# Two tables of partial neighbour sums in place of four in a graph kernel: each accumulating scatter waits for the second one ahead of it

## The chip, the cores and the metric

The kernel runs on one core of one Trainium2 chip. The metric is the device time of one execution in microseconds (us); before the change it is 12705.93 us, the median of 3 runs.

## The reference

12500 nodes of 128 features, 412500 edges sorted by `dst` (a self loop for each node among them), an `edge_weight` and 64 edge features for each edge. Two layers:

```
relevant = segment_sum(x[dst] * edge_weight[:, None], src, 12500)     # layer 0: the neighbour sums
x = layernorm(x + relevant @ W1 + (relevant * x) @ W2)
q, k, v = x @ Wq + bq, x @ Wk + bk, x @ Wv + bv                        # layer 1: attention, 8 heads
e = edge_attr_64 @ We + be
attn = softmax over the edges of each dst of (q[dst] . (k[src] + e)) / 4
x = layernorm(x + segment_sum(attn * v[src], dst) @ Wo + bo)
```

The neighbour sums of layer 0 are gathered by `dst` (sorted, so 128 edges in a row read a short window of `x`) and added up by `src` (random rows). That adding up is the part that the change touches.

## The kernel before, in words

Edges go in tiles of 128; eight tiles (`G`) are a group, and there are 403 groups (`NG`), so 3224 tiles. Five stages follow one another, each a block in which the engines run their own instruction streams and meet through semaphores.

**prepare** (L159 to L329) loads the edge arrays, derives the start row of each tile and the marks of the attention stage, and stores them. On SyncE's queue (L206 to L250) the order is: loads, `dst_pad` and its two shifted read-backs, then the zero fill of every table `rel_sum[r]` (L228 to L231: four transfers of `zeros` for each table), then `src_flat`, `starts`, `firsts`, `rel_flat`, the four `marks` and the two `whole`. The stage ends when all of them have landed (L250).

**neighbours** (L332 to L478) runs once over the 403 groups. For each group SyncE broadcasts the `src` values into `src_bc` (L375) and loads eight windows of `x` (L380). VectorE builds `same` and `spread` (L396, L400) and the eight columns of target rows, `row` (L414). TensorE multiplies them into `coef_ps` (L427), ScalarE copies it (L449), TensorE makes `sum_ps` (L436), ScalarE copies it into `sums` (L455). GpSimd then issues eight indirect DMAs (L471), one for each tile: 128 rows of 512 B from `sums[:, b, j]` are added to the rows of a table that `row[:, b, j]` names. Two of these may name the same row of the result, and an accumulating DMA reads its destination before it writes it, so two that may overlap in time must have different tables or be ordered. Scatter j goes to table j % REPLICAS, each table has its own semaphore `added[r]`, and before each scatter GpSimd waits until the one before it on the same table has landed. With four tables that is the scatter four ahead:

```
r, before = j % REPLICAS, j // REPLICAS
if j % 4 == 0:
    pool.wait_ge(sum_out, s.g * 2 + j // 4 + 1)
wait_alone(pool, added[r], (s.g * PER + before) * 16, passed)
pool.indirect_dma_start(out=rel_sum[r], ..., compute_op=ALU.add, ...).then_inc(added[r], 16)
```

`wait_alone` (L77 to L81) is a wait with a semaphore increment behind it; the wait and the increment are one instruction in the trace, under L81. The buffers `row` and `sums` are double: VectorE before L414 and ScalarE before L455 wait until all scatters of the group before the last have landed (L412, L451).

**nodes_one** (L528 to L676) goes over the nodes in 25 steps of 512. SyncE loads `xb` and a slice of each table into `rep` (L582, L584), VectorE adds the slices (L598, L599, L602), multiplies by `xb` (L605), and TensorE, ScalarE and VectorE make the layer norm and q, k, v. GpSimd stores them.

**attention** (L701 to L1168) is the long second pass over the 403 groups, and **nodes_two** (L1171 to L1264) ends the kernel. Neither touches the tables.

Of the kernel before, what the change touches and what calls it, by code (L numbers as in the profile page):

```python
# [25 lines left out]
ALU = mybir.AluOpType  # L26
# [2 lines left out]

P = 128  # L30
G = 8
REPLICAS = 4
BIG = 1.0e30
EPS = 1.0e-5
NB = 4 * P
# [34 lines left out]
def wait(eng, sem, value):  # L70

    if isinstance(value, int) and value <= 0:
        return
    eng.wait_ge(sem, value)  # L74
# [22 lines left out]
def build_gnn(nc, x, src, dst, edge_attr, edge_weight, W1, W2, Wq, bq, Wk, bk, Wv, bv, We, be, Wo, bo, out):  # L97
# [25 lines left out]
    firsts = nc.dram_tensor("firsts", (TP,), I32).ap()  # L123
    rel_sum = [nc.dram_tensor(f"rel_sum{r}", (N + P, D), F32).ap() for r in range(REPLICAS)]
    x1_rows = nc.dram_tensor("x1_rows", (N, D), F32).ap()
# [33 lines left out]
def prepare(nc, e):  # L159
# [13 lines left out]
    with ExitStack() as ctx:  # L173
# [24 lines left out]
        with nc.Block() as block:  # L198
# [7 lines left out]
            def _(sp):  # L206
# [20 lines left out]
                sp.wait_ge(zeroed, 1)  # L227
                for r in range(REPLICAS):  # L228
                    table = rel_sum[r].rearrange("n d -> (n d)").rearrange("(z p k) -> z p k", z=4, p=P)
# [15 lines left out]
                with nc.allow_non_contiguous_dma(reason="one word for each tile, once"):  # L245
# [3 lines left out]
                                 ).then_inc(prep_stored, 16)  # L249
                sp.wait_ge(prep_stored, 16 * (4 * REPLICAS + 10))  # L250

# [80 lines left out]
def neighbours(nc, e):  # L332
# [5 lines left out]
    with ExitStack() as ctx:  # L338
# [3 lines left out]
        def sem(name):  # L342
            return ctx.enter_context(nc.semaphore(name))
# [17 lines left out]
        coef_done, coef_out, sum_done, sum_out = (sem(n) for n in ("coef_done", "coef_out", "sum_done", "sum_out"))  # L361
        added = [sem(f"added{r}") for r in range(REPLICAS)]
        PER = G // REPLICAS

        with nc.Block() as block:
# [19 lines left out]
            def _(dve):  # L385
# [3 lines left out]
                def body(s):  # L389
# [21 lines left out]
                    dve.wait_ge(rows_b, s.g + 1)  # L411
                    for r in range(REPLICAS):  # L412
                        wait(dve, added[r], 16 * PER * (s.g - 1))
# [88 lines left out]
def layer_norm(nc, ch, i, passed, y, stats, mv, rstd, var_ready, rooted, out, done):  # L502

    for j in range(4):
        ch.mark(nc.vector.bn_stats(stats[:, j, :], y[:, j, :]))  # L505
    ch.settle()
    ch.eng.sem_inc(passed, 1)
    for j in range(4):
        ch.mark(nc.vector.bn_aggr(mv[:, j, :], stats[:, j, :]))  # L509
    ch.settle()  # L510
    nc.vector.tensor_scalar(rstd[:, 0, :], mv[:, :, 1], EPS, None, ALU.add).then_inc(var_ready, 1)  # L511
    ch.eng.wait_ge(rooted, i + 1)
    ch.link(nc.vector.reciprocal(rstd[:, 2, :], rstd[:, 1, :]))  # L513
    for j in range(4):
        nc.vector.tensor_scalar(out[:, j, :], y[:, j, :], mv[:, j, 0:1], rstd[:, 2, j:j + 1],  # L515
                                ALU.subtract, ALU.mult).then_inc(done, 1)


def node_steps(eng, N, body):

    full = N // NB
    body(0, 0)
    with eng.Fori(1, full) as i:  # L523
        body(i, i * NB)
    body(full, N - NB)


def nodes_one(nc, e):  # L528

    N, D = e["N"], e["D"]  # L530
# [3 lines left out]
    with ExitStack() as ctx:  # L534
        def sb(name, shape, dt=F32):
            return ctx.enter_context(nc.sbuf_tensor(name, shape, dt))
# [4 lines left out]
        def sem(name):  # L541
            return ctx.enter_context(nc.semaphore(name))
# [4 lines left out]
        xb = sb("xb", [P, 4, D])  # L547
        rep = sb("rep", [P, REPLICAS, 4 * D])
        pair = sb("pair", [P, 2, 4, D])
        half_sum = sb("half_sum", [P, 2, 4 * D])  # L550
        pair_t = sb("pair_t", [P, 2, 4, P])
        y = sb("y", [P, 4, D])
        stats = sb("stats", [P, 4, 6])
# [8 lines left out]
        w_in, bias_ready, in_x, summed, pair_turned, pair_out, y_done = (sem("n1_" + n) for n in (  # L562
            "w_in", "bias_ready", "in_x", "summed", "pair_turned", "pair_out", "y_done"))
        var_ready, rooted, x1_ready, x1_turned, x1_out, qkv_done, qkv_ready, stored, ch1 = (sem("n1_" + n) for n in (
            "var_ready", "rooted", "x1_ready", "x1_turned", "x1_out", "qkv_done", "qkv_ready", "stored", "chain"))
        CH = 2 + 1 + 4 + 4 + 1

        with nc.Block() as block:
            @block.sync
            def _(sp):  # L570
                for i, w in enumerate((e["W1"], e["W2"])):
                    sp.dma_start(w12[:, i, :], w).then_inc(w_in, 16)
                for i, w in enumerate((e["Wq"], e["Wk"], e["Wv"])):
                    sp.dma_start(wqkv[:, i, :], w).then_inc(w_in, 16)
                for i, b in enumerate((e["bq"], e["bk"], e["bv"], e["be"])):
                    sp.dma_start(bias[:, i, :], b.rearrange("(a d) -> a d", a=1).to_broadcast([P, D])
                                 ).then_inc(w_in, 16)

                def body(i, row0):
                    wait_alone(sp, x1_ready, i * 4, e["passed"])  # L580
                    rows = bass.ds(row0, NB)
                    sp.dma_start(xb[:], x[rows, :].rearrange("(p j) d -> p j d", j=4)).then_inc(in_x, 16)  # L582
                    for r in range(REPLICAS):
                        sp.dma_start(rep[:, r, :], rel_sum[r][rows, :].rearrange("(p j) d -> p (j d)", j=4)  # L584
                                     ).then_inc(in_x, 16)

                node_steps(sp, N, body)

            @block.vector
            def _(dve):  # L590
                dve.wait_ge(w_in, 9 * 16)
                nc.vector.tensor_tensor(bias[:, 1, :], bias[:, 1, :], bias[:, 3, :], ALU.add).then_inc(bias_ready, 1)
                dve.wait_ge(bias_ready, 1)

                def body(i, row0):
                    ch = Chain(dve, ch1, CH, i)
                    dve.wait_ge(in_x, (i + 1) * 16 * (1 + REPLICAS))
                    ch.mark(nc.vector.tensor_tensor(half_sum[:, 0, :], rep[:, 0, :], rep[:, 1, :], ALU.add))  # L598
                    ch.mark(nc.vector.tensor_tensor(half_sum[:, 1, :], rep[:, 2, :], rep[:, 3, :], ALU.add))  # L599
                    ch.settle()  # L600
                    wait(dve, pair_turned, i * 2)
                    nc.vector.tensor_tensor(pair[:, 0].rearrange("p j d -> p (j d)"), half_sum[:, 0, :],  # L602
                                            half_sum[:, 1, :], ALU.add).then_inc(summed, 1)
                    dve.wait_ge(summed, i * 2 + 1)
                    nc.vector.tensor_tensor(pair[:, 1], pair[:, 0], xb[:], ALU.mult).then_inc(summed, 1)  # L605
                    dve.wait_ge(y_done, i + 1)
                    ch.link(nc.vector.tensor_tensor(y[:], xb[:], y_ps[:], ALU.add))
                    wait(dve, stored, i * 48)
                    layer_norm(nc, ch, i, e["passed"], y, stats, mv, rstd, var_ready, rooted, x1, x1_ready)
                    for j in range(4):  # L610
                        dve.wait_ge(qkv_done, i * 4 + j + 1)
                        nc.vector.tensor_tensor(qkv[:, j], qkv_ps[j][:, 0:3, :], bias[:, 0:3, :], ALU.add
                                                ).then_inc(qkv_ready, 1)
                    ch.close()

                node_steps(dve, N, body)
# [554 lines left out]
def nodes_two(nc, e, acc):  # L1171

    N, D, x1_rows, out = e["N"], e["D"], e["x1_rows"], e["out"]
    with ExitStack() as ctx:
# [3 lines left out]
        def sem(name):  # L1178
# [15 lines left out]
            "w_in", "in_x", "att_ready", "y_done", "y_read", "var_ready", "rooted", "res_ready", "stored", "chain"))  # L1194
        CH = 1 + 1 + 4 + 4 + 1

        with nc.Block() as block:
# [13 lines left out]
            def _(dve):  # L1211
                dve.wait_ge(w_in, 32)

                def body(i, row0):
                    ch = Chain(dve, chain, CH, i)
                    nodes = bass.ds(row0, NB)
                    ch.link(nc.vector.reciprocal(inv[:], acc[:, 1, nodes]))  # L1217
                    wait(dve, y_done, i)
                    nc.vector.tensor_tensor(att[:], acc[:, 0, nodes], inv[:], ALU.mult).then_inc(att_ready, 1)  # L1219
                    dve.wait_ge(in_x, (i + 1) * 16)  # L1220
                    nc.vector.tensor_tensor(xo[:], xb[:], bo[:].rearrange("p (a d) -> p a d", a=1)
                                            .to_broadcast([P, 4, D]), ALU.add).then_inc(y_read, 1)
                    dve.wait_ge(y_read, i + 1)
                    dve.wait_ge(y_done, i + 1)
                    ch.link(nc.vector.tensor_tensor(y[:], xo[:], y_ps[:], ALU.add))  # L1225
                    wait(dve, stored, i * 16)
                    layer_norm(nc, ch, i, e["passed"], y, stats, mv, rstd, var_ready, rooted, res, res_ready)
                    ch.close()
# [58 lines left out]
```

## Time and profile before

| | us |
|---|---|
| median of 3 runs | 12705.93 (12699.51 to 12716.78) |
| span of the profiled execution | 12688.7 |
| of it: scatters, from the first to the last | 210.6 to 6201.4 |
| of it: nodes_one | about 6208 to 6740 |
| of it: attention | about 6740 to the last half per cent of the span |

The profiled execution has no time of its own beside its span; the span lies 17.2 us under the median of the runs. Busy shares of the whole span: TensorE's matmuls 66%, GpSimd 64%, VectorE 45%, ScalarE 35%. They are averages over stages with different limits: in the scatter stage TensorE is busy for about four tenths of each slice and GpSimd for eight, in the attention stage TensorE for nine tenths or more.

### The profile page before, as it was taken

The numbers are of one execution on the slowest core, as the hardware profiler recorded it, in microseconds if no ns is written. First come the engines' busy times: TensorE is split into PE (matmuls) and PEld (weight loads), VectorE is DVE, ScalarE is ACT, GpSimd is POOL, SyncE is SP. The second block draws the span as 40 slices with busy tenths as digits, with TensorE's granted clock in tenths as the row PEclk, the third lists the DMA queues.
The fourth block names the chain that finished last, engine by engine and source line by source line (L and its number), as shares of the span: only waits on it lengthen the run. The fifth ranks groups of instructions, "written<-read, shape, count | busy, mean of one in ns | idle before, by whom it ended". The sixth has DMA issues, their size and how long they took to land. (4 is left out here: it accounts for less than half of the span.)

```text
span 12688.7 us, 238906 instructions
## 1 busy us (share of the span) xinstructions
PE 8350.0 (66%) x54376; PEld 7719.8 (61%) x54376; DVE 5700.1 (45%) x23624; ACT 4480.1 (35%) x8672; POOL 8152.3 (64%) x6563
## 2 busy tenths in 40 slices
PE   2444444444444444444457999999999999999992
PEld 1343343443443343343336998999999989989892
DVE  2333333333333333333344555555555555555557
ACT  1111111111111111111104666666666666566660
POOL 2888888888888888888504555555555555555550
PEclk6666666666666666666657889999988898898995
DMA  7666666666666666666435666666666666666661
GB/s 199 105 106 106 105 106 106 105 106 106 105 106 106 105 106 106 105 106 106 95 114 157 178 177 181 178 179 182 180 176 179 176 181 179 175 181 175 182 182 50
DMA packets 2256479, 1764.21 MB, mean 139 GB/s; under 512 B 727631, under 2 KB 1990545, under 8 KB 2253937
## 3 DMA queue, kind: packets, MB, share of 16 engines
q0 software_dynamic: 628608, 667.05, 31.9%
q1 hardware_dynamic: 1627507, 1094.03, 30.0%
q14 instruction: 345, 2.83, 0.1%
q8 instruction: 19, 0.31, 0.0%
HBM read 1476.50 MB, written 283.60 MB: 139 GB/s over the span
## 5 line engine op out<-in xcount | busy, mean ns | idle before, releaser
L471 POOL DMA_INDIRECT rel_sum<-sums,row x3224 | 5008.9, 1554 | 1190.1 <-issue 648.9
L877 POOL DMA_INDIRECT kv<-kv_rows,src_idx x3224 | 3064.8, 951 | 2568.8 <-DVE msg L1076 1314.2
L427 PE MATMUL coef_ps<-same,spread 128*128 128x128 f32 x6448 | 1631.9, 437 | 3567.1 <-DVE spread L400 2963.4
L427 PEld LDWEIGHTS coef_ps<-same,spread 128*128 128x128 f32 x6448 | 1422.1, 325 | 3743.0 <-DVE spread L400 3129.2
L1090 DVE TENSOR_TENSOR acc<-acc,out_ps 128x256 f32 x3224 | 1335.4, 414 | 1050.2 <-PE out_ps L968 954.2
L414 DVE TENSOR_TENSOR row<-moved,src_col 128x8 int32<-128x8 f32 x403 | 70.3, 175 | 3787.2 <-DMA rel_sum<-sums,row 3787.1
L966 PE MATMUL out_ps<-put,msg 128*128 128x128 f32 x6448 | 1615.0, 340 | 88.9 <-DVE acc L1090 31.2
L968 PE MATMUL out_ps<-put,weight 128*128 128x128 f32 x6448 | 1516.1, 324 | 0.0
L455 ACT ACTIVATE sums<-sum_ps 128x512 f32<-128x512 f32 x806 | 437.7, 594 | 2895.4 <-DMA rel_sum<-sums,row 2893.9
L966 PEld LDWEIGHTS out_ps<-put,msg 128*128 128x128 f32 x6448 | 1243.2, 239 | 185.6 <-issue 77.3
L449 ACT ACTIVATE coef<-coef_ps 128x512 f32<-128x512 f32 x806 | 481.3, 597 | 2307.2 <-PE coef_ps L427 2306.1
L968 PEld LDWEIGHTS out_ps<-put,weight 128*128 128x128 f32 x6448 | 1247.8, 240 | 0.0
L400 DVE TENSOR_SCALAR spread<-iota_n,rel_col,w_col 128x128 f32<-128x128 f32 x3224 | 1213.1, 381 | 0.0
L396 DVE SCALAR_TENSOR_TENSOR same<-src_bc,src_col,later 128x128 f32<-128x128 f32 x3224 | 1119.2, 347 | 178.0 <-DVE row L414 163.2
L915 PE MATMUL ke_ps<-attr_t,we 128*128 128x128 f32 x6448 | 1096.0, 275 | 0.0
L915 PEld LDWEIGHTS ke_ps<-attr_t,we 128*128 128x128 f32 x6448 | 998.4, 195 | 0.0
L436 PE MATMUL sum_ps<-x_win,coef 128*128 128x128 f32 x6448 | 996.3, 320 | 0.0
L436 PEld LDWEIGHTS sum_ps<-x_win,coef 128*128 128x128 f32 x6448 | 995.8, 242 | 0.0
L1123 ACT ACTIVATE put<-iota_n,neg_rel 128x128 f32<-128x128 f32 x3224 | 981.1, 387 | 0.0
L913 PE MATMUL ke_ps<-ident,kv 128*128 128x128 f32 x3224 | 902.8, 280 | 7.8 <-ACT attr_t L1132 7.8
L924 PE MATMUL misc_ps<-head_of,prod 128*128 128x8 f32 x6448 | 842.9, 259 | 95.6 <-DVE prod L1001 95.6
L924 PEld LDWEIGHTS misc_ps<-head_of,prod 128*128 128x128 f32 x6448 | 815.2, 199 | 135.2 <-DVE prod L1001 107.8
(151 smaller groups left out, 10350.2 us busy)
## 6 DMA issues: line engine op xcount, KB each, us to landing
src_bc<-src_flat SPq DMA_DIRECT2D x403, 512.0 KB, 4.2
x_win<-in_x SPq DMA_DIRECT2D x3224, 64.0 KB
rel_bc<-rel_flat SPq DMA_DIRECT2D x403, 512.0 KB
q_win<-q_rows SPq DMA_DIRECT2D x3224, 64.0 KB
attr<-in_edge_attr SPq DMA_DIRECT2D x402, 256.0 KB
rel_sum<-sums,row POOLq DMA_INDIRECT x3224, 3.4
kv<-kv_rows,src_idx POOLq DMA_INDIRECT x3224
mark<-marks SPq DMA_DIRECT2D x403, 128.0 KB
```

The source lines that it names most:

```text
L396: nc.vector.scalar_tensor_tensor(out=same[:, b, j, :], in0=src_bc[:, b, j * P:(j + 1) * P], scalar=src_col[:, t], in1=later[:], op0=ALU.is ...
L400: nc.vector.tensor_scalar(spread[:, b, j, :], iota_n[:], rel_col[:, t], w_col[:, t], ALU.is_equal, ALU.mult).then_inc(masks, 1)
L427: last = nc.tensor.matmul(coef_ps[k][:, i, :], spread[:, b, j, :], same[:, b, j, :], start=True, stop=True)
L436: last = nc.tensor.matmul(sum_ps[k][:, i, :], coef[:, b, j, :], x_win[:, b, j, :], start=True, stop=True)
L471: pool.indirect_dma_start(out=rel_sum[r], out_offset=bass.IndirectOffsetOnAxis(ap=row[:, b, j:j + 1], axis=0), in_=sums[:, b, j, :], in_of ...
L877: pool.indirect_dma_start(out=kv[:, b3, j, :], out_offset=None, in_=kv_rows, in_offset=bass.IndirectOffsetOnAxis(ap=src_idx[:, b3, j:j + 1 ...
L915: mm = nc.tensor.matmul(ke_ps[k][:, i, :], we2[:, j % 2, :], attr_t[:, j // 2, :], start=False, stop=True)
L924: mm = nc.tensor.matmul(logit_ps[:, j * H:(j + 1) * H], prod[:, j * P:(j + 1) * P], head_of[:], start=True, stop=True)
L966: nc.tensor.matmul(out_ps[p2 % 2][:, i, 0, :], msg[:, j, :], put[:, c.turn(2), j, :], start=True, stop=True)
L968: mm = nc.tensor.matmul(out_ps[p2 % 2][:, i, 1, :], weight[:, j, :], put[:, c.turn(2), j, :], start=True, stop=True)
L1090: nc.vector.tensor_tensor(win, win, out_ps[j // 2 % 2][:, j % 2, :, :], ALU.add).then_inc(summed, 1)
L1123: nc.scalar.activation(put[:, n.turn(2), j, :], iota_n[:], ACT.Abs, bias=neg_rel[:, bass.ds(n.g * G + j, 1)]).then_inc(put_dist, 1)
```

## The change

`REPLICAS` goes from 4 to 2. What follows from it in the code: two tables are zeroed in place of four (8 transfers on SyncE's queue in place of 16); scatter j goes to table j % 2, so it waits for the scatter two ahead of it; `PER`, the scatters of a group on one table, goes from 2 to 4; `nodes_one` loads two slices of tables in place of four, and one addition in place of three makes the sum.

```
-REPLICAS = 4
+REPLICAS = 2
...
-        half_sum = sb("half_sum", [P, 2, 4 * D])
...
-        CH = 2 + 1 + 4 + 4 + 1
+        CH = 1 + 4 + 4 + 1
...
                     dve.wait_ge(in_x, (i + 1) * 16 * (1 + REPLICAS))
-                    ch.mark(nc.vector.tensor_tensor(half_sum[:, 0, :], rep[:, 0, :], rep[:, 1, :], ALU.add))
-                    ch.mark(nc.vector.tensor_tensor(half_sum[:, 1, :], rep[:, 2, :], rep[:, 3, :], ALU.add))
-                    ch.settle()
                     wait(dve, pair_turned, i * 2)
-                    nc.vector.tensor_tensor(pair[:, 0].rearrange("p j d -> p (j d)"), half_sum[:, 0, :],
-                                            half_sum[:, 1, :], ALU.add).then_inc(summed, 1)
+                    nc.vector.tensor_tensor(pair[:, 0].rearrange("p j d -> p (j d)"), rep[:, 0, :],
+                                            rep[:, 1, :], ALU.add).then_inc(summed, 1)
```

## Rows read from the trace of the kernel before

**Rows 1.** The page: span; costliest groups (busy us, mean ns, idle before and its releaser).

```profile
span 12688.7 us, 238906 instructions
...
L471 POOL DMA_INDIRECT rel_sum<-sums,row x3224 | 5008.9, 1554 | 1190.1 <-issue 648.9
...
L455 ACT ACTIVATE sums<-sum_ps 128x512 f32<-128x512 f32 x806 | 437.7, 594 | 2895.4 <-DMA rel_sum<-sums,row 2893.9
```

**Rows 2.** Windows: the scatter stage, nodes_one, attention and the end.

```profile
210.00:6205.00 5995.00, 2542.01 (x12864) 2366.63 (x12864) 1947.44 (x10843) 916.98 (x1609) 5008.88 (x3224) 0.67 0.62 105
6208.00:6740.00 532.00, 301.19 (x900) 197.98 (x900) 205.93 (x576) 51.20 (x101) 50.60 (x77) 0.59 0.34 112
6740.00:12688.00 5948.00, 5485.87 (x40502) 5140.40 (x40502) 3488.52 (x12140) 3493.83 (x6880) 3089.64 (x3256) 0.88 0.63 172
```

**Rows 3.** Timeline of one group's middle: start, duration, engine, line, idle before.

```profile
2727.56 1.59 POOL L471 DMA_INDIRECT rel_sum<-sums,row  x1 [0.30 <-issue]
2729.45 1.55 POOL L471 DMA_INDIRECT rel_sum<-sums,row  x1 [0.30 <-issue]
...
2730.82 0.33 SPq L375 DMA_DIRECT2D src_bc<-src_flat  x1
...
2731.31 1.55 POOL L471 DMA_INDIRECT rel_sum<-sums,row  x1 [0.30 <-DMA rel_sum<-sums,row]
```

**Rows 4.** Line L471, 1000 to 6000 us: duration ns, first and last start, landing.

```profile
L471 POOL DMA_INDIRECT rel_sum<-sums,row x2691: 1542/1548/1698, 998.6 to 5999.1; - x193
...
DMA to landing us min/median/max: 3.2/3.4/6.1
```

**Rows 5.** Line L471 in four windows of one scatter: starts 2725.7, 2729.5, 2733.2, 2736.9.

```profile
L471 POOL DMA_INDIRECT rel_sum<-sums,row x1: 1544/1544/1544, 2725.7 to 2725.7; - x1
DMA to landing us min/median/max: 3.3/3.3/3.3
...
L471 POOL DMA_INDIRECT rel_sum<-sums,row x1: 1550/1550/1550, 2729.5 to 2729.5; - x1
DMA to landing us min/median/max: 4.5/4.5/4.5
...
DMA to landing us min/median/max: 3.2/3.2/3.2
...
DMA to landing us min/median/max: 3.5/3.5/3.5
```

**Rows 6.** Line L81 on GpSimd's queue, 2733.5 to 2736: when waits are passed.

```profile
L81 POOLq EVENT_SEMAPHORE  x2: 17/17/17, 2734.0 to 2735.5; - x2
```

**Rows 7.** A gather of the attention stage: the wait passed, then its start.

```profile
L81 POOLq EVENT_SEMAPHORE  x1: 17/17/17, 7999.8 to 7999.8; - x1
...
8000.57 0.95 POOL L877 DMA_INDIRECT kv<-kv_rows,src_idx  x1 [3.03 <-DVE msg L1076]
```

**Rows 8.** Line L471 from 208 to 216 us: first issue and first scatters.

```profile
L471 POOLq MOVE  x4: 29/29/29, 209.6 to 211.6; - x4
L471 POOL DMA_INDIRECT rel_sum<-sums,row x3: 1552/1569/1901, 210.6 to 214.6; - x3
```

**Rows 9.** prepare: SyncE's queue and VectorE in order of time; transfers of zeros.

```profile
48.65 34.48 SPq L231 DMA_DIRECT2D rel_sum<-zeros  x16
...
86.48 33.42 SPq L235 DMA_DIRECT2D starts<-start_ti  x1
...
140.33 19.51 SPq L243 DMA_DIRECT2D marks<-mark_t  x4
...
84.30 7.07 DVE L297 TENSOR_TENSOR_SCAN mark_t<-next_t,mark_t 128x3328 f32<-128x3328 int32 x1
...
rel_sum<-zeros SPq DMA_DIRECT2D x16, 1578.5 KB, 27.9
...
GB/s 0 0 79 317 313 278 143 157 43 295 352 447 414 432 417 432 419 429 419 429 417 434 414 354 91 2 2 0 221 348 348 348 348 95 1 1 0 0 341 90
```

**Rows 10.** nodes_one on VectorE by line: busy, mean ns, idle before.

```profile
L599 DVE TENSOR_TENSOR half_sum<-rep 128x512 f32<-128x512 f32 x25 | 17.1, 685 | 0.0
L598 DVE TENSOR_TENSOR half_sum<-rep 128x512 f32<-128x512 f32 x25 | 17.0, 682 | 3.0 <-DMA rep<-rel_sum 3.0
```

## The prediction, made before the changed kernel had run

> **What bounds the kernel now.** I read the page's costliest groups first, then the windows by stage, then the timeline of one group and the landing times of single scatters. The stages run one after the other, so each has a limit of its own. The change touches prepare, the scatter stage and nodes_one, not attention, which is TensorE's: 5486 of its 5948 us are matmuls [rows 2]. I expect attention unchanged.
>
> In the scatter stage GpSimd is busy 5009 of 5995 us and nothing else comes near it [rows 2]. The reader should see what its idle time is: before nearly every scatter stands the same 0.30 us, put down to issue or to a landing that falls into that gap, and one scatter starts 1.85 us after the other, which is 1.55 of duration and 0.30 of gap [rows 3]. The mean over the stage is 1.859 us: the first scatter starts at 210.6 [rows 8], the last of the 3224 at 6201.4 (the table of times), and 5990.8 / 3223 = 1.859. A group of eight takes 14.87 us. The others wait for the scatters: ScalarE's copy into `sums` stands idle 2894 us for landings [rows 1], about 7 us for each of the 403 groups. So GpSimd's own instruction rate is the limit, and the landings are not: the waits on `added` are met early.
>
> How early decides this case. A scatter lands 3.4 us after its start by the median, never under 3.2, at most 6.1 [rows 4]. With four tables, scatter i waits for one that started 4 x 1.859 = 7.4 us before it. That leaves 4.0 us, in which GpSimd's queue runs ahead: at 2734.0 the wait on the scatter of 2729.45 is passed, 4.5 us after that one's start and 2.9 us before the scatter behind the wait starts, at 2736.9 [rows 3, 5, 6].
>
> **The change part by part.**
>
> (a) The wait. Now scatter i waits for the landing of i-2. The cost is not landing against 2 x 1.859 = 3.72 us alone: between the passing of a wait and the start of the DMA behind it lies the time in which the queue handles the instruction. Today the queue has that time in hand; with the wait ending late it stands in line with the landing. The trace of before doesn't show it for a steady scatter. The nearest rows: a gather with GpSimd idle starts at 8000.57, 0.8 us after its wait was passed at 7999.8 [rows 7]; the first scatter starts 1.0 us after its register move (209.6 to 210.6), which itself follows the wait by up to 0.1 [rows 8]. So it is between 0.8 and 1.1 us. I take 0.9, the gather's value and the register move that a scatter has in addition; the first scatter also ran long (1.90 against 1.55 us), so it looks like a cold start.
>
> A pair of scatters then costs landing + 0.9, where today it costs 3.72. In a quiet stretch: 3.3 + 0.9 = 4.2 us. Not all are quiet: of the four scatters in rows 5 the landings are 3.3, 4.5, 3.2 and 3.5 us. The 4.5 is that of the scatter that started at 2729.45, while SyncE issued the 512 KB broadcast `src_bc` at 2730.82 [rows 3]; the scatter behind it, started at 2731.31, was late as well, its wait being passed at 2735.5, so 4.2 us [rows 6]. There is one such broadcast and one burst of eight window loads in each group, before and after the change.
>
> The scatters form two chains, one for each table: tiles 1, 3, 5, 7 and tiles 0, 2, 4, 6. The odd chain takes 14.5 us of landings (3.3 + 4.5 + 3.2 + 3.5) and 4 x 0.9 = 3.6, together 18.1 us for each group. The even one has the 4.2 and three of about 3.4: 14.4 + 3.6 = 18.0. They share GpSimd, and which is the later one changes, so I add an estimated 0.2: 18.3 us against 14.87. For 403 groups: 3.43 x 403 = +1382 us. With 0.8 in place of 0.9 it would be 161 less (4 x 0.1 x 403), with 1.1 it would be 322 more.
>
> What is queued behind the waiting scatter: GpSimd's queue holds nothing but the next scatters. Who waits for them: `row` and `sums` need the landing of the last scatter of the group before the last. They get it one group ahead of use; ScalarE's 2894 us of idle show 7 us of slack in each group [rows 1], and a group that takes 18.3 us makes that slack longer. SyncE's loads wait for VectorE and TensorE, which move with them. So nothing new comes late, and PE's, VectorE's and ScalarE's work stays hidden under the scatters.
>
> The Trainium skill, "DMA: Bandwidth & Descriptors", section "Anatomy of one DMA", gives a DMA issued by GpSimd as about 2.0 us plus its bytes over 436 GB/s, an estimated 2.15 us for 64 KB. Counted from issue, 2.15 + 0.9 is under 3.72 and (a) would cost nothing; the trace has no landing under 3.2 us [rows 4], so it disagrees. Counted from the end of the 1.55 us on GpSimd, it would be 3.7 us, 0.4 above the quiet landings here, and (a) would cost 4 x 0.4 x 403 = 645 us more than my sum; the trace has 3.4 - 1.55 = 1.85.
>
> (b) The zero fill. 16 transfers of 1578.5 KB; DMA moves some 425 GB/s in that stretch, so 3.8 us each [rows 9]. SyncE's queue is in line behind them: `starts` needs 33.4 us to issue, because the queues are full [rows 9]. Eight fewer: -30.4 us. It is on the path, since the stage ends with the last transfer of that queue. The next limit is VectorE's last scan, which ends at 91.4, while the marks are issued at 140.3 and would then be at 109.9 [rows 9]: still behind it, so all 30 us are kept.
>
> (c) nodes_one. VectorE's two additions of 0.68 us go from each of 25 steps, with their settling wait: 2 x 0.68 = 1.37, and about 0.04 for the wait [rows 10]. They are on the path, because they stand right behind the q, k, v additions of the step before with no idle (only 3.0 us in all 25, in the first step). The loads of `rep` are hidden under that step but in the first one, where two fewer issues save about 1. Together -36 us. The least it can be is 0, if a load of `rep` landed as late as the additions end now; the 3.0 us of idle in 25 steps speak against that.
>
> Sum against the profiled execution: 12688.7 + 1382 - 30 - 36 = 14,005 us of span; with the 17 us between span and median, 14,022. I forecast 14,020 us, 10.3% slower.
>
> **The rivals.**
>
> *The wait stays hidden (not slower).* If a wait that ends late needed only the 0.30 us that stands before each scatter now, the link in a quiet stretch would be 3.3 + 0.3 = 3.6 us, under 3.72, and GpSimd's rate would remain the limit; the broadcasts' excess would have to be made up too, by other landings. Then only (b) and (c) count: 12706 - 66 = 12,640 us. For it: the 0.30 is all that a reader sees between scatters [rows 3]. Against it: the 0.8 of the gather [rows 7] and a 4.5 in every group, which by itself leaves 4.5 + 0.3 - 3.72 = 1.1 us. It decides from landing plus handling at 3.72. Chance 0.03.
>
> *The broadcasts don't hurt.* With fewer scatters in flight and a longer period, the late landings might fade to the quiet 3.3. Pair 4.2, scatter 2.1 us: (2.1 - 1.859) x 3224 = +777, less 66: 13,417 us. For it: most landings are quiet. Against: the broadcast is as large as before and one comes in each group. Chance 0.14.
>
> *The chains hurt each other, or handling is as long as the first scatter shows.* With 1.1 us: 19.1 us for a group, +1705 - 66: 14,345. Or with 0.9, where the late landing of one chain also holds up the other by its 0.9 excess: 19.2, 14,385. Chance 0.16.
>
> The likeliest is my sum with its neighbours, from 13,860 (handling 0.8) to 14,250, halfway to the case above: 0.66. 0.01 is left for something that I don't see.
>
> **How the numbers follow.** All cases but the first are slower by over 0.2% (about 25 us, what a measurement of this kernel can tell from no change): slower 0.96. The first is faster: 0.03, and 0.01 for same. The range: 0.2 may stay out. The hidden case (0.03) does, and so do the lower half of the fading case and the upper part of the last: 13,400 to 14,400 us.
>
> **What the profile of the changed kernel would show.** For (a): the scatters' duration still 1.55 us, but idle before them 0.7 us and more, released by landings of `rel_sum`; starts 4.2 us apart for every second one and 18.3 us for a group; the stage 7375 us long; GpSimd busy 68% of it in place of 84%. Right or wrong on the handling time: wait passed to start, 0.9. For (b): first scatter at about 180. For (c): nodes_one 36 us shorter. Attention at 5948. I would be wrong if that idle stayed at 0.30, if landings under the slower rate became much shorter than 3.3, or if the late ones spread to the whole group.

## The result, and the profile after

The changed kernel takes 13944.75 us (median of 3 runs, 13942.82 to 13958.27) against 12705.93: a ratio of 1.0976, 95% interval 1.0961 to 1.0991, slower. The forecast was 14,020.

The page of the changed kernel: the span, the two groups that answer to [rows 1], and the scatters' issue with its median landing.

```profile
span 13956.6 us, 238726 instructions
...
L471 POOL DMA_INDIRECT rel_sum<-sums,row x3224 | 5007.8, 1553 | 2505.6 <-issue 1175.2
...
L455 ACT ACTIVATE sums<-sum_ps 128x512 f32<-128x512 f32 x806 | 437.7, 594 | 4199.6 <-DMA rel_sum<-sums,row 4198.3
...
rel_sum<-sums,row POOLq DMA_INDIRECT x3224, 3.3
```

The scatters' own time did not move (5009 to 5008 us, 1.55 us each), nor did their median landing (3.4 and 3.3 us; those views hold half of the tiles each, and over all of them it is 3.40 and 3.35). The idle time before them more than doubled, from 1190 to 2506 us. Without the wait before the very first scatter (207 and 178 us) it is 984 and 2327 us: that difference, 1344 us, is the loss of the stage. ScalarE's copy into `sums` waits 4198 us instead of 2894: it has more slack, not less, as a follower of the scatters should.

Windows of the changed kernel (the scatter stage, nodes_one, attention). The columns, as in [rows 2]: stretch and its length; busy us and instructions of TensorE's matmuls, its weight loads, VectorE, ScalarE and GpSimd; granted clock of TensorE, busy share of the DMA engines, GB/s.

```profile
182.00:7518.00 7336.00, 2558.66 (x12864) 2367.05 (x12863) 1931.61 (x10840) 916.93 (x1609) 5007.83 (x3224) 0.64 0.51 86
7520.00:7970.00 450.00, 250.50 (x900) 162.99 (x900) 173.99 (x526) 51.20 (x101) 50.26 (x75) 0.74 0.32 103
8030.00:13685.00 5655.00, 5453.40 (x40164) 5123.03 (x40162) 3272.71 (x11664) 3469.74 (x6823) 3036.28 (x3200) 0.89 0.65 177
```

Beside [rows 2]: GpSimd is busy 5008 of 7336 us, 68%, where it was 84%. In nodes_one TensorE was granted 0.74 of its full clock, where it was 0.59. That I had not foreseen.

The timeline of one group's middle shows where the idle sits; compare [rows 3], where it was 0.30 us everywhere.

```profile
3014.75 1.59 POOL L471 DMA_INDIRECT rel_sum<-sums,row  x1 [0.80 <-DMA rel_sum<-sums,row]
3016.15 0.33 SPq L375 DMA_DIRECT2D src_bc<-src_flat  x1
3016.64 1.54 POOL L471 DMA_INDIRECT rel_sum<-sums,row  x1 [0.30 <-issue]
3020.20 1.55 POOL L471 DMA_INDIRECT rel_sum<-sums,row  x1 [2.01 <-DMA rel_sum<-sums,row]
...
3022.05 1.54 POOL L471 DMA_INDIRECT rel_sum<-sums,row  x1 [0.30 <-issue]
3024.51 1.55 POOL L471 DMA_INDIRECT rel_sum<-sums,row  x1 [0.92 <-DMA rel_sum<-sums,row]
```

The landing of the first of these alone, and GpSimd's wait on it (line L81):

```profile
L471 POOL DMA_INDIRECT rel_sum<-sums,row x1: 1587/1587/1587, 3014.8 to 3014.8; - x1
...
DMA to landing us min/median/max: 4.6/4.6/4.6
...
L81 POOLq EVENT_SEMAPHORE  x1: 17/17/17, 3019.4 to 3019.4; - x1
```

These lines show the mechanism. The scatter of 3014.75 has the broadcast of `src_bc` issued on top of it at 3016.15 and lands after 4.6 us. At that moment, 3019.4, the wait behind it is passed, and the next scatter on its table starts at 3020.20, 0.8 us later. From the start of one scatter to the start of the next on its table, which I call a link, it is 5.45 us; with four tables the same late landing cost nothing. In the quiet link after it, 3020.20 to 3024.51, it is 4.31 us instead of 3.72. The scatter in between (3022.05) starts 1.85 us behind its neighbour: GpSimd's own rate (1.55 us of duration and 0.30 of gap) still spaces the two that come together, and idle gathers before every second one. In this group the late scatter is tile 2; in most groups it is tile 3, as over all 403 groups tile 2 lands after 3.35 us by the median and tile 3 after 4.54.

The issues of line L471 over the whole run, with their first and last start, and the landings:

```profile
L471 POOL DMA_INDIRECT rel_sum<-sums,row x3224: 1537/1547/1836, 182.5 to 7515.9; - x190
...
DMA to landing us min/median/max: 3.1/3.3/5.3
```

(7515.9 - 182.5) / 3223 = 2.275 us for a scatter, 18.20 us for a group, against 1.859 and 14.87.

By stage, both profiled executions (the times are the starts of the first and last scatter of line L471 and of the first and last of attention's additions into `acc`):

| us | before | after | difference | forecast |
|---|---|---|---|---|
| to the first scatter | 210.6 | 182.5 | -28 | -30 |
| first to last scatter | 5990.9 | 7333.4 | +1343 | +1382 |
| last scatter to attention's first addition | 600.7 | 514.3 | -86 | -36 |
| attention, first to last addition | 5614.4 | 5654.5 | +40 | 0 |
| to the end | 272.1 | 272.0 | 0 | 0 |
| span | 12688.7 | 13956.6 | +1268 | +1316 |

The medians differ by 1239 us, 29 less than the spans. The last 272 us are nodes_two, which is 2% of the span and not the half per cent that the table of times before gave it. The 40 us of attention can't be laid to the change: that stage took 5614 to 5655 us in nine profiled executions of kernels that are alike in it, the changed kernel itself 5630 in another. But the three of them with the fast scatter stage took 5614 to 5621 us and the six with a slower one 5622 to 5655, so that a small effect is not excluded either.

### The profile page after: what moved, and what is told of

It reads as the page before. It is cut to its first block and busy times, and to the rows that moved or that the text cites. A ratio compares the mean times of both kernels' runs of the same rounds, so it can differ in the third digit from the quotient of the medians.

```text
span 13956.6 us, 238726 instructions
## 1 busy us (share of the span) xinstructions
PE 8363.3 (60%) x54376; PEld 7738.0 (55%) x54376; DVE 5653.7 (41%) x23574; ACT 4481.0 (32%) x8672; POOL 8145.9 (58%) x6563
## 5 line engine op out<-in xcount | busy, mean ns | idle before, releaser
L471 POOL DMA_INDIRECT rel_sum<-sums,row x3224 | 5007.8, 1553 | 2505.6 <-issue 1175.2
```

The source lines that it names most:

```text
L471: pool.indirect_dma_start(out=rel_sum[r], out_offset=bass.IndirectOffsetOnAxis(ap=row[:, b, j:j + 1], axis=0), in_=sums[:, b, j, :], in_of ...
```

## The experiments

Eleven runs follow: nine kernels, one of them twice, and the changed kernel once more. Four of them (the wait alone, nodes_one alone, the zero fill undone and three tables) ran together on a chip on which attention took 8350 us instead of some 5640, so that the kernel before took 15432.57 us there (median of 17 runs); their scatter stages and steps of nodes_one agree with those on the other chips to within half a per cent where the kernels are alike in them. Why attention is slow there is open. These four are compared with the kernel before on the same chip, and stage by stage.

**The wait alone.** Four tables, with the wait moved to the second scatter ahead:

```
-                        wait_alone(pool, added[r], (s.g * PER + before) * 16, passed)
+                        wait_alone(pool, added[(j - 2) % 4], (s.g * PER + (j + 2) // 4) * 16, passed)
```

> Four tables as before the change, but each scatter also waits for the landing of the second one ahead of it: part (a) alone. The wait on the fourth one ahead is replaced, since the nearer wait covers it in order. My theory (a link is landing plus a fixed 0.86 us of handling): the scatter stage grows as in the changed kernel, by some 1340 us, to 18.2 us for a group; zero fill and nodes_one as before; 14,050 us. Rival 1: part of the stage's loss comes of two scatters in a row hitting the same two tables, not of the wait; then the stage here is shorter than 18.0 us for a group, under 13,970. Rival 2: nodes_one's gain in the changed kernel (20.4 to 17.1 us a step) comes from what the slower scatter stage does to TensorE's clock; then its step is shorter here too, about 18.5, and the time about 14,000.

Measured: 16783.57 us, ratio 1.0879 (1.0863 to 1.0895), +1351 us. The scatter stage took 7337 us, 18.21 us for a group. Once more, beside the changed kernel on one ordinary chip:

> Part (a) alone once more, beside the changed kernel on one chip. Theory: before plus 1345 us; the scatter stage 7335 us, nodes_one's step 20.4 us; above the changed kernel by the 28 us of prepare and the 85 us of nodes_one, some 110 us. Rival: the two tables themselves matter and the difference is not between 90 and 130.

> The changed kernel as it is, on the same chip as the other three: before plus 1240 us (ratio 1.0976 on another occasion).

Measured: before 12718.62 (11 runs), the wait alone 14106.84 (ratio 1.1088, 1.1070 to 1.1107), the changed kernel 13986.62 (ratio 1.1003, 1.0984 to 1.1023). The wait alone on that chip, by its scatters and by nodes_one from 7603 to 8095 us:

```profile
L471 POOL DMA_INDIRECT rel_sum<-sums,row x3224: 1536/1546/1872, 213.4 to 7581.3; - x190
...
7603.00:8095.00 492.00, 290.66 (x868) 189.42 (x868) 197.79 (x554) 49.19 (x97) 48.24 (x72) 0.58 0.34 114
```

The scatter stage is 7368 us with four tables and 7377 with two (7563.5 - 186.3) on the same chip. So the wait makes the loss; that the same two tables are hit in turn adds no more than the 9 us between these traces. The two kernels differ by 120 us, where prepare and nodes_one should make some 110. The medians of the changed kernel on the two occasions, 13945 and 13987, show how far chips differ; the ratios overlap.

**nodes_one alone.** Two slices loaded and added, all else with four tables, so that the output lacks the sums of the other two:

```
-                    for r in range(REPLICAS):
+                    for r in range(2):
                         sp.dma_start(rep[:, r, :], rel_sum[r][rows, :]...
```

> Four tables, all zeroed and scattered to as before, but nodes_one reads and adds two of them only, as in the changed kernel (the output lacks the sums of the other two tables): part (c) alone. My prediction's theory: two additions fewer, 1.4 us a step, 36 us in all, 12,670 us. Rival, from the trace after: the shorter wait of TensorE lets its clock rise, so that the step falls from 20.4 to about 17.1 us whatever ran before it: 85 us in all, 12,620 us. A third: the clock depends on what ran before, and the step is between 18.5 and 19.5.

Measured: 15377.99 us, ratio 0.9970 (0.9956 to 0.9983), 55 us less, the interval reaching from 26 to 68. By the time alone this lies between the theory's 36 and the rival's 85; the stage tells more. VectorE's product in nodes_one (25 times, first and last start) and the window between, for the kernel before, the changed one and this one, each its own answer:

```profile
L605 DVE TENSOR_TENSOR pair<-pair,xb x25: 691/692/693, 6223.1 to 6713.2; 128x512 f32<-128x512 f32 x25
...
6223.00:6713.00 490.00, 289.02 (x864) 190.12 (x864) 197.16 (x553) 49.20 (x97) 47.98 (x72) 0.60 0.35 114
```

```profile
L601 DVE TENSOR_TENSOR pair<-pair,xb x25: 691/691/693, 7536.7 to 7946.9; 128x512 f32<-128x512 f32 x25
...
7537.00:7947.00 410.00, 240.71 (x865) 156.98 (x865) 166.55 (x505) 49.21 (x97) 46.93 (x71) 0.75 0.33 106
```

```profile
L601 DVE TENSOR_TENSOR pair<-pair,xb x25: 691/692/693, 6220.8 to 6631.6; 128x512 f32<-128x512 f32 x25
...
6222.00:6632.00 410.00, 242.01 (x863) 157.71 (x863) 166.54 (x504) 49.20 (x97) 47.25 (x71) 0.75 0.33 106
```

A step is 490.1 / 24 = 20.4 us before, 410.2 / 24 = 17.1 after, and 17.1 here, with the fast scatter stage ahead of it. With the slow scatter stage and four slices it stays at 20.5 and a clock of 0.58 (the wait alone, above). So the step and the clock go with what nodes_one itself does, not with what ran before. Its 24 steps are 80 us shorter than those of the wait alone on the same chip; attention took 8369 us there against 8346, and that takes back most of what the time lacks.

**The zero fill undone.** The changed kernel, with eight more transfers of zeros into two spare tables.

> The changed kernel, but with four tables' worth of zeros written as before, two of them to tables that nothing uses: part (b) undone. My theory: prepare ends some 28 to 30 us later, the rest is as in the changed kernel: 13,974 us. Rival: the first scatter's earlier start has another reason and nothing moves: 13,945.

Measured: 16737.31 us, ratio 1.0845 (1.0829 to 1.0860). The first scatter starts at 209.8 us instead of 182.5, so the zero fill is worth 27 us. The time alone could not tell: it is 1305 us over before, with an interval of some 24 us to each side, where +1267 would follow. Of the 38 us too many, 24 are in the scatter stage (7357 us against 7333) and the rest is not traced.

**One table.** `REPLICAS = 1`, and one copy in place of the additions.

> One table: each scatter waits for the landing of the one just ahead of it, and nodes_one copies one slice. My theory: a scatter costs its landing plus 0.855 us of handling; with the mean landing of the changed kernel, 3.52 us, 4.375 us each, 14,106 us for the stage against 7336, and some 30 us less around it: 20,690 us. Rival: with one scatter in flight nothing delays the landings and all are quiet (3.28): 4.14 us each, 19,900 us. Another: the handling is partly hidden behind GpSimd's idle: under 3.6 us each, under 18,200 us.

Measured: 20459.12 us (one run). Three scatters in a row:

```profile
3618.95 1.54 POOL L471 DMA_INDIRECT rel_sum<-sums,row  x1 [2.63 <-DMA rel_sum<-sums,row]
3619.03 0.34 SPq L375 DMA_DIRECT2D src_bc<-src_flat  x1
3624.09 3.94 SPq L380 DMA_DIRECT2D x_win<-in_x  x8
3624.30 1.55 POOL L471 DMA_INDIRECT rel_sum<-sums,row  x1 [3.81 <-DMA rel_sum<-sums,row]
3628.62 1.54 POOL L471 DMA_INDIRECT rel_sum<-sums,row  x1 [2.78 <-DMA rel_sum<-sums,row]
```

The stage takes 13,884 us, 4.31 us a scatter, 222 us less than the theory's 14,106. The theory had 4.375 and the rival of quiet landings 4.14, so it lies nearer to the theory: over all scatters of the trace the mean landing is 3.43 us, as the broadcast and the window loads still make some late, but less so than with two in flight (3.52). Nothing of the handling is hidden: in this trace, in that of the changed kernel and in the two below, the time from the last semaphore increment of a landing to the start of the scatter that waited for it is 0.855 us at the median, and within 0.02 of that for nine in ten of those that waited.

**The broadcast twice, and the windows left out.**

```
                                  .to_broadcast([P, GP])).then_inc(src_in[b], 16)
+                    sp.dma_start(src_more[:, b, :], ...).then_inc(src_in[b], 16)
```

The second transfer has the source of the first and a buffer that nothing reads. In the other kernel, all groups but the first two multiply by windows that are out of date:

```
-                    for j in range(G):
-                        sp.dma_start(x_win[:, b, j, :], x[bass.ds(start[j], P), :]).then_inc(x_in[b], 16)
+                    if isinstance(s.u, int) and s.g < 2:
+                        for j in range(G):
+                            sp.dma_start(x_win[:, b, j, :], x[bass.ds(start[j], P), :]).then_inc(x_in[b], 16)
```

> The changed kernel, but the 512 KB broadcast of src_bc is loaded a second time in each group, into a buffer that nothing reads, and VectorE waits for both. My theory: the broadcast makes the one landing of 4.5 us in each group, 1.2 us over a quiet one; two of them make it some 2.4 us, or a second scatter late: +1.2 us for a group, +480 us, 14,430 us (14,250 to 14,600). Rival: the late landing has another cause (window loads, the rows themselves): under +100 us.

> The changed kernel without the eight loads of x windows in all groups but the first two (later groups multiply by stale windows). My theory: the burst only adds 0.2 to 0.3 us to the landings of tiles 5 and 6, so the odd chain gains about 0.25 us for a group: -100 us, 13,840 us, and the landing of 4.5 us stays. Rival: the window loads make the 4.5: it falls to 3.3 and a group to about 17 us, 13,450 us.

Measured: 14551.46 us with two broadcasts, 13832.6 without window loads (one run each). With two broadcasts:

```profile
2639.86 1.54 POOL L474 DMA_INDIRECT rel_sum<-sums,row  x1 [0.63 <-issue]
2640.35 0.34 SPq L376 DMA_DIRECT2D src_bc<-src_flat  x1
2640.78 0.38 SPq L378 DMA_DIRECT2D src_more<-src_flat  x1
2641.74 1.55 POOL L474 DMA_INDIRECT rel_sum<-sums,row  x1 [0.34 <-issue]
...
2646.99 1.54 POOL L474 DMA_INDIRECT rel_sum<-sums,row  x1 [3.71 <-DMA rel_sum<-sums,row]
```

Its landings for the scatters of 2639.86 and 2641.74:

```profile
DMA to landing us min/median/max: 6.3/6.3/6.3
...
DMA to landing us min/median/max: 4.8/4.8/4.8
```

A group takes 19.69 us, 1.5 us or 601 us in all more than with one broadcast (480 expected). Without the windows it takes 17.90, 0.3 us less, 120 us in all (100 expected). Both are set against the first trace of the changed kernel, from another chip; its stage was 44 us longer in its second. A second broadcast makes the late landing later, by 1.6 us in the mean (4.45 to 6.03) rather than 1.2, and that behind it became late too (3.31 to 4.40); the landing stays late without the window loads (4.42). So the late landing in each group is the broadcast's doing, and the eight window loads matter little. A kernel without any broadcast was not run.

**Three tables.** Scatter t of the whole run goes to table t % 3; GpSimd waits for the third ahead.

> Three tables: a scatter waits for the third one ahead. My theory: it has 3 x 1.859 = 5.58 us, more than a landing of 4.5 and 0.86 of handling (5.36), so nearly every wait stays hidden and the stage keeps 14.9 us for a group; a quarter of the zero fill goes (15 us) and one addition of 0.7 us in each of 25 steps (18 to 45 us with the clock): 12,640 to 12,675 us, slightly faster than four tables. Rival: landings over 4.7 us are common enough (the maximum was 6.1) to cost more than that: the stage grows by over 60 us and the time is 12,700 or more.

Measured: 15567.07 us, ratio 1.0085 (1.0072 to 1.0098), 134 us more than before on that chip. My theory missed and the rival holds: the stage is 6150 us (1.908 us a scatter), 159 more. Its waits between 1000 and 6000 us:

```profile
POOL rel_sum L476 <- issue: 525.1, 1658, 2.2
POOL rel_sum L476 <- DMA rel_sum<-sums,row: 409.3, 963, 1.6
```

Waits reach 2.2 us where none was over 0.64 in that stretch before. The trace tells where the loss sits: 154 of the 159 us are idle before tile 6, the scatter that waits for tile 3, in 241 of the 403 groups. What I had wrong is the landing of tile 3, the scatter under the broadcast. Its median is 5.1 us here (by the last increment that this trace holds, as it lacks some), 4.5 both before and in the changed kernel, and 5.1 + 0.86 exceeds the 5.58 of three periods. But the 4.5 was a median of widely spread landings: in the kernel before, tile 3 took 3.3 to 5.6 us in nine groups of ten, and in 180 of the 403 over 4.72, which is all that three periods leave beside 0.86 of handling. So the trace of before already spoke for the rival. The landing goes with the moment of the broadcast: in the kernel before it is 5.3 us by the median where the broadcast was issued 1.3 us after the scatter's start (90 groups), 4.6 at 1.4 us (133) and 3.65 at 1.6 us (65).

**A version that beats both.** The nodes_one finding can be had without giving up a table: load the slices one step ahead and do the two additions while VectorE waits for TensorE. (`add_halves` waits for the slices and adds the first two and the last two.)

```
+                    if ahead is not None:
+                        wait_alone(sp, halves, i * 2 + 2, e["passed"])
+                        slices(ahead)
...
                     nc.vector.tensor_tensor(pair[:, 1], pair[:, 0], xb[:], ALU.mult).then_inc(summed, 1)
+                    if more:
+                        add_halves(i + 1)
                     dve.wait_ge(y_done, i + 1)
```

> Four tables and their waits as before the change; in nodes_one the two additions of table slices for the next step are issued while VectorE waits for TensorE's y, and the slices are loaded one step ahead, so that the part of a step between q, k, v and the transposes is as short as in the changed kernel. My theory (the gap before the transposes sets TensorE's granted clock, and with it the step): the step falls from 20.4 to about 17.1 us, 85 us in all, before minus 85 (12,620 where before is 12,706). Rival 1: the loads of half the data also mattered: about 19 us a step, minus 36. Rival 2: the additions don't fit where they are put and hold up y: minus 0 to 20.

> The same, and in prepare only one table is zeroed ahead of the stores of starts, firsts and the marks; the other three are zeroed behind them, while the slow word-by-word stores drain. My theory: DMA stood idle for some 40 us in prepare around those stores, and the zeros fill that: 20 to 40 us less than the kernel with hidden additions alone, the first scatter at 170 to 190 us. Rival: the word stores run on the same queues and are held up by the zeros just as long: 0.

Measured: 12623.76 us with hidden additions, ratio 0.9933 (0.9919 to 0.9946); 12631.71 with three of the four tables zeroed behind the stores of prepare as well, the same ratio. nodes_one with hidden additions:

```profile
L623 DVE TENSOR_TENSOR pair<-pair,xb x25: 691/693/693, 6226.0 to 6637.1; 128x512 f32<-128x512 f32 x25
...
6226.00:6640.00 414.00, 243.62 (x879) 159.72 (x880) 197.78 (x554) 50.43 (x99) 48.33 (x72) 0.75 0.41 136
```

The step is 17.1 us at a clock of 0.75 with all four slices still loaded (136 GB/s instead of 106) and all three additions still done (VectorE 198 us). So neither less data nor less work on VectorE brought the gain, but only that the additions no longer stand between TensorE's q, k, v and its next transposes. Moving the zeros brought nothing that the time shows: the first scatter starts at 213.5 us instead of 215.5. DMA traffic in 5 us slices from 0 to 200 us:

```profile
GB/s 0 0 77 311 312 289 166 140 34 301 368 444 417 429 335 26 1 1 36 85 320 348 347 348 223 2 16 94 192 439 419 429 417 427 422 429 419 177 213 130
```

Beside [rows 9], the empty slices only stand earlier (75 to 95 and 125 to 135 us), with the zeros behind them at 417 to 439 GB/s. The stores of single words (`starts`, `firsts`) still hold up what is queued behind them: from 75 to 95 us nearly nothing moves, while `firsts` and `rel_flat` are being issued.

## Why the prediction was right, point by point

- **The bound and its slack.** GpSimd's rate bound the stage, and the landings were met early; the change turned that into landing plus handling. Right: scatter duration and landing stayed, idle took all of the loss, and nothing behind the scatters became late. The waiting alone, with four tables, costs the same.
- **Handling, 0.9 us** between 0.8 and 1.1. Measured 0.855: the gather was the better row, and the 1.1 of the first scatter is not the value of the steady ones. The 0.045 too much, four times a group, would make 73 us; the next two terms gave 32 of them back.
- **Landings of the odd chain, 14.5 us.** Means over all groups of the changed kernel, read from the trace: 3.30, 4.45, 3.51 and 3.29 for tiles 1, 3, 5, 7, together 14.55. That it came so close has luck in it. The four values were those of a single group, and the 4.5 could have been any from 3.3 to 5.6 us there; tile 5 rose from 3.2 to 3.51 as tile 7 fell from 3.5 to 3.29. The even chain got 13.6 instead of 14.4: its tile 4 lands at 3.31, no longer 4.2; it now starts 2.0 us after the issue of the broadcast by the median, where it was 0.5. So in the mean the odd chain sets the group, and the other has 0.9 us to spare.
- **The 0.2 us for chains holding each other.** 14.55 + 4 x 0.855 = 17.97, measured 18.20: 0.23. The whole group, 18.3, was 0.1 too high: +1343 us instead of +1382.
- **Zero fill, -30.** -28 between the traces, 27 when undone. SyncE's queue now stands from 60.8 to 63.75 us, before `src_flat`, until VectorE ends a pass over the marks at 63.7, a wait that I had not looked at; whether it cost the 2 us is not shown. The issue of `starts` behind the zeros took 24.6 us with eight transfers ahead of it, 33.4 with sixteen and 9.3 with four.
- **nodes_one, -36.** Mis-sized: -86 in the profile, 80 of it in 24 steps that are 3.3 us shorter each, instead of 1.4. I took the two additions off the step and left TensorE's durations as they were; they fell with the higher granted clock, from 289 to 241 us of matmuls in the two windows of the 24 steps, which is 2.0 us a step. That the shorter gap on TensorE's side raises the clock is shown by hidden additions (same gap, all the work) and by nodes_one alone.
- **Attention and end.** Unchanged within what runs differ by.
- **The rivals.** The hidden wait is excluded by 0.855 in place of 0.30 and by the one-table kernel, where a scatter costs its landing and the handling in full. Fading broadcasts are excluded by the changed kernel itself, where tile 3 lands after 4.45 us in the mean. The last case is excluded in both forms, by 0.855 instead of 1.1 and by 18.20 us for a group instead of 19.1 or 19.2. (Its edge was also misplaced: halfway from 14,020 to 14,345 or 14,385 is some 14,190, not 14,250.) By "Anatomy of one DMA" in the Trainium skill's "DMA: Bandwidth & Descriptors" a DMA of 64 KB issued by GpSimd takes an estimated 2.15 us; the traces have 3.3 from issue and 1.75 (3.3 - 1.55) from the end of GpSimd's part, so the page fits neither way of counting, the second better.

Against the spans the forecast was 48 us too high: 39 in the scatter stage and 50 in nodes_one, less 40 of attention and 2 of prepare. The remaining 27 of its 75 us lie between the profiled executions and the medians.

## What to carry to other kernels

When a ring of buffers or tables is made shorter, compare the period of the ring with landing plus handling, not with landing alone: a queue that runs ahead hides the handling, and a wait that ends late shows it. Use the landing that comes late once in each round, and its spread rather than its median, and expect it to shift when the rhythm changes. Where TensorE works in bursts between waits, look at the granted clock before costing a step: work taken out of its gaps may bring more than its own time (3.3 us a step for 1.4 here).

## What the runs showed of the hardware, beyond what I had expected

- The time from a landing's last semaphore increment to the start of the waiting accumulate scatter is 0.855 us, the same in four kernels to within 0.02 for nine in ten of the scatters that waited.
- How late a scatter under the 512 KB broadcast lands goes with tenths of a microsecond between the two: 5.3 us where the broadcast was issued 1.3 us after the scatter's start, 3.65 where it was 1.6.
- Shortening a 20.4 us step by 1.4 us of VectorE work raised TensorE's granted clock in nodes_one from 0.60 to 0.75 (of 2.4 GHz; the levels are 1.2 and 2.4) and the step fell to 17.1 us. With three tables it was 0.62 and 19.5 us.
- One chip ran attention, and only attention, in 8350 us instead of 5640, in all four kernels tried there. The cause is open.
